# Four graph layers over sorted edges: record loads by several steps, stores of end rows by four, a relation loop with six buffers

## The chip, the cores and the metric

The kernel runs on one core of a Trainium2 chip. The metric is the device time of one execution in microseconds (us), the median over several executions. Beside it stands one profiled execution, whose records say what each engine did and waited for. Engines are named as in the profile: PE (TensorE, matmuls), DVE (VectorE), ACT (ScalarE), POOL (GpSimd) and SP (SyncE); PEq, SPq, ACTq are their instruction queues.

## The reference

A graph has 3125 nodes with 256 features and 103125 edges (50000 in both directions and a loop at each node). Four layers follow each other, each on `h = relu(layernorm(x))` and each added to `x`:

```python
x = x + _L0_gnn_ref(h, edge_index, edge_attr_18, ...)            # 16 heads; k and q get a projection of the attributes
x = x + _L1_gnn_ref(h, edge_attr_64, edge_weight, edge_index, ...)  # 8 heads, edge projection, then a feed-forward block
x = x + _L2_gnn_ref(h, weight, gamma, beta, src, dst, edge_type_8)
x = x + _L3_gnn_ref(h, src, dst, W, attn_l, attn_r, bias)        # 4 heads, additive attention, leaky relu
```

Layers 0, 1 and 3 are attention: for every edge a score per head from both ends' rows, a softmax over the edges that share a node, and the sum of the weighted value rows over those edges. Layer 2 is a sum without softmax, then a batch norm:

```python
all_h = jnp.einsum('ni,rio->nro', h, weight)      # eight relations: a table of 8 rows per node
msg = all_h[src, rel]
agg = jax.ops.segment_sum(msg, dst, num_segments=h.shape[0])
```

## The kernel before

**Stages.** The kernel sorts the edges on the chip by source and by destination and writes a *record* for each into two lists in memory, `by_src_records` and `by_dst_records` (node numbers, table index, attributes, weight). Then come, one after the other with a barrier of all engines between them: the layer loops `edges0` (over the list by source), `edges1`, the relation loop and `edges3` (over the list by destination), and between them stages that join the sums, project `x` and write the tables of the next layer. All loops have their instructions in program order on each engine; semaphores alone tie the engines together, and there is no planner.

**A step.** The sorted list has T = 856 tiles of 128 edges, and a step is G = 8 tiles, so that each loop has STEPS = 107 steps. Two tiles are a pair; a step has PAIRS = 4. Nodes lie in blocks of BN = 126 rows, NB = 25 blocks, joined in GROUPS = 5 groups of 5. A pair's edges belong to one block of nodes, whose number DVE loads into a register (`blocks_of`).

**Relation loop (`relation_sums`).** SP loads the step's records (L1684, 128 partitions x 8 tiles x 8 words). POOL gathers, tile by tile, 128 rows of 256 values from the table `rel` into `rows` (L1693, eight indirect DMAs a step). DVE makes eight one-hot matrices 128x128 from the records (L1724). PE multiplies, two tiles into one PSUM bank for each pair (L1709, 8 matmuls a step), and DVE adds the pair's PSUM to `acc` (printed as `agg`, L1741). The order is kept by these semaphores: `rec_in[b]` (records there), `gathered[b][h]` (half a step's rows there), `hot_ready` (one-hots there), `summed` (PE, one increment per pair) and `added` (DVE, one per pair). With BUFS2 = 3 buffers SP waits at step n, before it loads, until `summed` says that step n - 3 is finished. POOL waits for nothing but `rec_in`, so its buffer of rows is guarded through SP's wait. PE waits before each pair's matmuls until DVE has added the pair three before, since the PSUM banks are four.

**Layer loops (`edge_layer`, kind 0, 1, 3).** The same outline with more work: SP loads the records (L1137) into `rec`, one of BUFS = 4 buffers, after `score_done` of the step four before; POOL gathers rows of keys and values (L1152) when the records are there and PE has finished the step four before; ACT, DVE and PE make one-hots, scores, exponentials and weighted rows; PE sums them by pairs (L1262, kind 1 L1273); ACT copies the sums out of PSUM (L1411, L1415, in `move_sums`), and once a step stores the two *end rows* of each pair, which belong to nodes that the next block of edges also has, into `ends` (L1418), having waited with `ends_out` for the store before. The loops are unrolled by 12 steps.

**Others.** In the sort, SP loads the attributes of each step (L539) into the records that POOL then scatters. After it, SP loads the segment words of the first and the last edge of each tile (L920, 28 DMAs). In each joining stage SP loads the sums of segments that were cut between tiles, `far`, block by block (L1844 in `load_parts`, 25 DMAs of 128 rows; 126 of them are the block's, the last two those of the next).

## Time and profile before

| what | us |
|---|---|
| median of 3 executions | 9863.49 (9828.07 to 9897.71) |
| the profiled execution | 9902.93 |
| its span in the profile | 9901.2 |
| edges0, edges1, relation loop, edges3 (stretches) | 1720, 1549, 1299, 1354 |
| busy over the span: PE, DVE, POOL, ACT | 6502.3, 5118.9, 5166.4, 3754.8 |

The stages can't overlap, so each loop's length is set by the engine or the wait that ends last in it, and the busy times over the whole span say little. "Idle before" in a row is the time that the engine stood still just before the instruction; what ended it is inferred from semaphore events, and a wait for a *count* of a semaphore (as `summed` is) can be put down to a wrong instruction, here several times to "DMA edges_kv<-kv,edges_rec", a gather of an earlier stage. "issue" is idle time that ended with nothing that the profile shows. The granted clock of PE was 0.779 over the span; 0.5 is 1.2 GHz and 1.0 is 2.4 GHz.

### The profile page before, as it was taken

To read this page: it belongs to the slowest core of one execution; us is meant where nothing else is said; L and a number is where in the kernel's file an instruction comes from. 1 tells how busy PE (TensorE), PEld (TensorE's weight loads), DVE (VectorE), ACT (ScalarE), POOL (GpSimd) and SP (SyncE) were. 2 spreads that over 40 slices of the span, in tenths; PEclk is the share of its full clock that TensorE was granted. 3 is DMA by queue.
4 is the path that set the end of the run, shared out by engine and by line. 5 is a ranking of instruction groups with operands and counts; after the bars stand their busy time and mean duration, and the time that the engine had idled before them with its cause. 6 is when DMAs were issued, how large, how long until landed. Compare 5 with 4: busy or idle time off the path is not lost. (4 is left out here: it accounts for less than half of the span.)

```text
span 9901.2 us, 144141 instructions
## 1 busy us (share of the span) xinstructions
PE 6502.3 (66%) x32549; PEld 4796.2 (48%) x32550; DVE 5118.9 (52%) x15163; ACT 3754.8 (38%) x11176; POOL 5166.4 (52%) x5189
## 2 busy tenths in 40 slices
PE   8555555666556777777578888879644545566664
PEld 7554444445444555555356655656433334344443
DVE  6665555555545555565577777741122223344445
ACT  3221112222224555555266666744100001566663
POOL 0565555666655445555156656530366663566664
PEclk9666766666768889899789999989766666677776
DMA  7310002111114334444255555542333333333333
GB/s 222 88 13 12 13 12 60 27 27 27 26 23 106 101 103 105 107 108 105 91 156 157 158 152 161 161 113 65 85 91 90 88 90 71 85 89 88 89 90 75
DMA packets 1047506, 873.99 MB, mean 88 GB/s; under 512 B 755175, under 2 KB 863893, under 8 KB 1046843
## 3 DMA queue, kind: packets, MB, share of 16 engines
q0 software_dynamic: 259600, 655.15, 24.4%
q1 hardware_dynamic: 731943, 158.23, 8.2%
q10 hardware_dynamic: 55428, 54.63, 1.7%
q8 instruction: 195, 3.19, 0.1%
q14 instruction: 340, 2.79, 0.1%
HBM read 733.43 MB, written 134.17 MB: 88 GB/s over the span
## 5 line engine op out<-in xcount | busy, mean ns | idle before, releaser
L1152 POOL DMA_INDIRECT edges_kv<-kv,edges_rec x1712 | 1826.7, 1067 | 1474.7 <-issue 728.1
L1262 PE MATMUL banks<-edges_kv,edges_hot 128*128 128x288 f32 (+2 forms) x5136 | 1716.7, 489 | 739.5 <-DVE edges_kv L1536 630.5
L1262 PEld LDWEIGHTS banks<-edges_kv,edges_hot 128*128 128x128 f32 x5136 | 1159.5, 236 | 1121.9 <-ACT edges_pair_sums L1415 344.1
L558 POOL DMA_INDIRECT by_src_records<-sort_by_src_rec,sort_pos_i x808 | 783.1, 969 | 801.9 <-DVE sort_pos_i L625 553.6
L699 PE MATMUL banks<-sort_table,sort_hot_hi_t 128*128 128x128 f32 x3232 | 862.9, 405 | 422.1 <-DVE sort_junk L643 246.7
L1693 POOL DMA_INDIRECT edges_rows<-rel,edges_rec x856 | 810.3, 947 | 588.8 <-DMA edges_rec<-by_dst_records 319.8
L1152 POOL DMA_INDIRECT edges_kv<-feat,edges_rec x856 | 821.7, 960 | 538.9 <-issue 329.9
L1709 PE MATMUL banks<-edges_rows,edges_hot 128*128 128x256 f32 x1712 | 624.2, 530 | 678.2 <-DVE agg L1741 284.8
L558 POOL DMA_INDIRECT by_dst_records<-sort_by_dst_rec,sort_pos_i x808 | 783.1, 969 | 541.1 <-DVE sort_pos_i L625 329.9
L643 DVE SCALAR_TENSOR_TENSOR sort_junk<-banks,sort_hot_lo 128x128 bf16<-128x128 f32 x1616 | 439.0, 286 | 1083.4 <-remote 737.5
L699 PEld LDWEIGHTS banks<-sort_table,sort_hot_hi_t 128*128 128x128 f32 x3232 | 670.8, 284 | 504.6 <-DVE sort_junk L643 290.2
L1709 PEld LDWEIGHTS banks<-edges_rows,edges_hot 128*128 128x128 f32 x1712 | 433.0, 265 | 869.5 <-issue 420.1
L1380 ACT ACTIVATE edges_off<-columns,edges_column 128x128 bf16<-128x128 f32 x2568 | 784.5, 390 | 0.0
L577 ACT COPY sort_hot_hi_t<-banks 25x512 f32<-25x512 f32 x404 | 232.3, 575 | 1335.2 <-remote 732.6
L1352 ACT ACTIVATE edges_apart<-banks,minus_p 128x512 bf16<-128x512 f32 x642 | 429.8, 686 | 700.5 <-DMA sort_feat<-in_edge_attr_dram 298.8
L1741 DVE TENSOR_TENSOR agg<-banks,agg 128x256 f32 x428 | 181.1, 423 | 986.1 <-DMA edges_kv<-kv,edges_rec 541.7
L694 PE MATMUL banks<-sort_hot_lo,sort_hot_hi 128*128 128x128 bf16 x1616 | 293.1, 277 | 530.1 <-ACT sort_table L598 515.0
L635 DVE SCALAR_TENSOR_TENSOR sort_junk<-banks,sort_key_cur,sort_earlier 128x128 bf16<-128x128 f32 x1616 | 576.3, 412 | 5.8 <-PE banks L678 5.8
L1569 DVE TENSOR_TENSOR edges_kv<-banks,edges_kv 128x256 f32<-128x256 f32 (+1 forms) x856 | 448.9, 553 | 186.3 <-remote 84.5
L1222 PE MATMUL banks<-x,edges_hot_t 128*128 x1712 | 496.6, 415 | 54.8 <-issue 41.0
L1554 DVE TENSOR_TENSOR edges_kv<-banks,edges_kv 128x256 f32<-128x256 f32 x428 | 179.1, 420 | 673.2 <-PE banks L1222 403.9
L1536 DVE TENSOR_TENSOR edges_kv<-edges_kv 128x1024 f32<-128x1024 f32 x428 | 519.8, 1215 | 3.9 <-ACT edges_kv L1397 3.9
(438 smaller groups left out, 12933.3 us busy)
## 6 DMA issues: line engine op xcount, KB each, us to landing
edges_kv<-kv,edges_rec POOLq DMA_INDIRECT x1712
sort_feat<-in_edge_attr_dram SPq DMA_DIRECT2D x100, 256.0 KB, 3.3
rel<-tables_stage SPq DMA_DIRECT2D x100, 252.0 KB
by_dst_records<-by_dst_blank ACTq DMA_DIRECT2D x1, 17120.0 KB
edges_rec<-by_dst_records SPq DMA_DIRECT2D x107, 160.0 KB
edges_rows<-rel,edges_rec POOLq DMA_INDIRECT x856
edges_kv<-feat,edges_rec POOLq DMA_INDIRECT x856
by_src_records<-sort_by_src_rec,sort_pos_i POOLq DMA_INDIRECT x808
```

Of the source, the lines that this page charges most:

```text
L558: pool.indirect_dma_start(O.rec, bass.IndirectOffsetOnAxis(ap=pos_i[:, b, c:c + 1], axis=0), rec[:, b, c, :], None).then_inc(scattered[b], 16)
L635: last = dve.scalar_tensor_tensor(out=junk[:, c, 0:P + mates].rearrange("p (t e) -> p t e", e=P), in0=ps[:, 4 + h, end - P - mates:end].re ...
L643: dve.scalar_tensor_tensor(out=junk[:, c, 2 * P:3 * P], in0=ps[:, 2 + c % 2, 0:P], scalar=1.0, in1=hot_lo[:, u, c, :], op0=ALU.mult, op1=A ...
L699: pe.matmul(ps[:, 2 + c % 2, 0:P], hot_hi_t[:, u, c, :], table[:, d % 2, :], start=True, stop=True).then_inc(looked_up, 1)
L1152: pool.indirect_dma_start(kv[:, r, c, 0:koff + DIM], None, tab, bass.IndirectOffsetOnAxis(ap=reci[:, r, c, idx:idx + 1], axis=0)).then_inc ...
L1222: last = pe.matmul(out[:, c, 2 * P - QW:2 * P], hot_t[:, b % 2, 2 * m + c, :], rows, start=(kind == 1), stop=(kind == 1 or c == 1), skip_g ...
L1262: last = pe.matmul(ps[:, 6 + m % 2, 0:OW], hot[:, b % 2, c, :], kv[:, b % BUFS, c, koff:koff + OW], start=(c % 2 == 0), stop=(kind != 1 an ...
L1380: last = act.activation(off[:, c, :], C.columns[:, c % 2, :], ACT.Abs, bias=column[:, b % 2, c:c + 1], scale=-1.0)
L1536: dve.tensor_tensor(v4, v4, bc(exps, dh), ALU.mult).then_inc(msg_done, 1)
L1569: dve.tensor_tensor(k2, by, k2, ALU.mult).then_inc(edges_used, 1)
L1693: pool.indirect_dma_start(rows[:, b, c, :], None, tab, bass.IndirectOffsetOnAxis(ap=reci[:, b, c, idx:idx + 1], axis=0)).then_inc(gathered ...
L1709: last = pe.matmul(ps[:, m, 0:DIM], hot[:, b, c, :], rows[:, b, c, :], start=(c % 2 == 0), stop=(c % 2 == 1))
```

## The change

- **Relation loop.** BUFS2 goes from 3 to 6, so that `rec` and `rows` hold six steps. SP loads the records of three steps in one DMA (LOAD = 3), for a group whose first step is n as soon as step n - 4 is finished (`n + 3 - 6` steps counted). PE increments `step_summed` once a step in place of `summed` once a pair, and waits for `added` once a step: three sets of PSUM (`sum_of`: two pairs in one bank, six banks) stand where four banks stood. The one-hots have three sets (SETS) and DVE makes them two steps ahead.
- **Layer loops.** `rec` holds twelve steps, loaded four at once (LOAD = 4). `pair_sums` holds four steps (HELD = 4), and the end rows of four steps are stored in one DMA.
- **Sort.** The attributes of two steps are loaded by one DMA, after a wait for both steps' scatters.
- **Head columns.** 10 DMAs in place of 28.
- **Joins.** `load_parts` loads a group's five blocks with one DMA of 126 partitions; POOL clears partitions 96 to 127 of `far` beforehand.

```diff
-BUFS, BUFS2 = 4, 3
+BUFS, BUFS2 = 4, 6
...
-                        for tile, q, lag in ((K.seg_head, 0, 0), (K.seg_prev, P - 1, 1)):
...
-                                sp.dma_start(tile[p0:p0 + last - first, k:k + 1],
-                                             seg_word[q, first:last].rearrange("(t o) -> t o", o=1)).then_inc(head_in[i], 16)
+                        whole = (TB - 1) * P
+                        sp.dma_start(K.seg_head[:, 0:TB - 1], seg_word[0, 0:whole].rearrange("(k p) -> p k", p=P)).then_inc(head_in[i], 16)
+                        sp.dma_start(K.seg_head[0:TLAST, TB - 1:TB], seg_word[0, whole:T].rearrange("(t o) -> t o", o=1)).then_inc(head_in[i], 16)
+                        sp.dma_start(K.seg_prev[1:P, 0:1], seg_word[P - 1, 0:P - 1].rearrange("(t o) -> t o", o=1)).then_inc(head_in[i], 16)
+                        sp.dma_start(K.seg_prev[:, 1:TB - 1], seg_word[P - 1, P - 1:whole - 1].rearrange("(k p) -> p k", p=P)).then_inc(head_in[i], 16)
+                        sp.dma_start(K.seg_prev[0:TLAST, TB - 1:TB], seg_word[P - 1, whole - 1:T - 1].rearrange("(t o) -> t o", o=1)).then_inc(head_in[i], 16)
...
     LO_BANKS = (3, 3) if kind < 3 else (3, 2)
     SEG_BANK = {0: 4, 1: 0, 3: 5}[kind]
     UNROLL = 12
+    LOAD = 4
     ENDS = 96
+    HELD = 4
     ROUNDS = -(-STEPS // UNROLL)
...
-        rec = ph.sbuf("rec", [P, BUFS, G, RW])
+        rec = ph.sbuf("rec", [P, UNROLL, G, RW])
...
-        pair_sums = ph.sbuf("pair_sums", [P, PAIRS, OW])
+        pair_sums = ph.sbuf("pair_sums", [P, HELD, PAIRS, OW])
...
-                    if not first_steps(j, b, BUFS):
-                        sp.wait_ge(score_done, at(j, b)(1, 1) - BUFS)
-                    sp.dma_start(rec[:, b % BUFS], records[:, bass.ds(j * (UNROLL * G) + b * G, G), word0:O.width]).then_inc(rec_in[b % BUFS], 16)
+                    if b % LOAD:
+                        return
+                    some = min(LOAD, size(j) - b)
+                    if not first_steps(j, b, UNROLL):
+                        sp.wait_ge(score_done, at(j, b)(1, some) - UNROLL)
+                    sp.dma_start(rec[:, b:b + some].rearrange("p s c w -> p (s c) w"),
+                                 records[:, bass.ds(j * (UNROLL * G) + b * G, some * G), word0:O.width]).then_inc(rec_in[b // LOAD], 16)
...
-                    pool.wait_ge(rec_in[r], turn_of(j, b) * 16 + 16)
+                    pool.wait_ge(rec_in[b // LOAD], j * 16 + 16)
...
-                    if 0 in pairs:
-                        act.wait_ge(ends_out, n(16, 0))
+                    if 0 in pairs and b % HELD == 0:
+                        act.wait_ge(ends_out, j * (UNROLL // HELD * 16) + b // HELD * 16)
...
-                    if PAIRS - 1 in pairs:
+                        act.copy(pair_sums[:, b % HELD, m, :], ps[:, 6 + m % 2, 0:OW]).then_inc(sums_copied, 1)
+                    if PAIRS - 1 in pairs and (b % HELD == HELD - 1 or b == size(j) - 1):
+                        held = b % HELD + 1
                         act.wait_ge(sums_copied, n(PAIRS, PAIRS))
-                        act.dma_start(ends_rows[:, bass.ds(n(PAIRS, 0), PAIRS), :], pair_sums[BN:P]).then_inc(ends_out, 16)
+                        act.dma_start(ends_rows[:, bass.ds(at(j, b + 1 - held)(PAIRS, 0), held * PAIRS), :],
+                                      pair_sums[BN:P, 0:held].rearrange("p s m w -> p (s m) w")).then_inc(ends_out, 16)
...
+    SETS = 3
+    LOAD = 3
+    IOTA = 7
...
+    def opening(j, b, n):
+
+        return isinstance(j, int) and j * BUFS + b < n
...
+    def sum_of(b, m):
+
+        return ps[:, 2 * (b % SETS) + m // 2, DIM * (m % 2):DIM * (m % 2) + DIM]
...
-                    sp.wait_ge(summed, (j * BUFS + b) * PAIRS - (BUFS - 1) * PAIRS) if not (isinstance(j, int) and j == 0) else None
-                    sp.dma_start(rec[:, b], records[:, bass.ds(j * (BUFS * G) + b * G, G), word0:O.width]).then_inc(rec_in[b], 16)
+                    if b % LOAD:
+                        return
+                    some = min(LOAD, (FINAL if isinstance(j, int) and j == ROUNDS - 1 else BUFS) - b)
+                    if not opening(j, b, BUFS):
+                        sp.wait_ge(step_summed, at(j, b)(1, some) - BUFS)
+                    sp.dma_start(rec[:, b:b + some].rearrange("p s c w -> p (s c) w"),
+                                 records[:, bass.ds(j * (BUFS * G) + b * G, some * G), word0:O.width]).then_inc(rec_in[b // LOAD], 16)
...
                     n = at(j, b)
+                    if not opening(j, b, SETS):
+                        pe.wait_ge(added, n(PAIRS, 0) - (SETS - 1) * PAIRS)
                     pe.wait_ge(hot_ready, n(1, 1))
                     for m in range(PAIRS):
                         if m % 2 == 0:
                             pe.wait_ge(gathered[b][m // 2], j * 64 + 64)
-                        if not (isinstance(j, int) and j == 0 and b == 0):
-                            pe.wait_ge(added, n(PAIRS, m) - (PAIRS - 1))
                         for c in (2 * m, 2 * m + 1):
-                            last = pe.matmul(ps[:, m, 0:DIM], hot[:, b, c, :], rows[:, b, c, :],
+                            last = pe.matmul(sum_of(b, m), hot[:, b % SETS, c, :], rows[:, b, c, :],
                                              start=(c % 2 == 0), stop=(c % 2 == 1))
-                        last.then_inc(summed, 1)
+                    last.then_inc(step_summed, 1)
...
                 def one_hot(j, b):
 
-                    if not (isinstance(j, int) and j == 0):
-                        dve.wait_ge(summed, at(j, b)(PAIRS, 0) - (BUFS - 1) * PAIRS)
-                    dve.wait_ge(rec_in[b], j * 16 + 16)
-                    dve.tensor_tensor(hot[:, b], ps[:, 7, 0:P].unsqueeze(1).to_broadcast([P, G, P]), bc(rec[:, b, :, lo], P),
+                    if not opening(j, b, SETS):
+                        dve.wait_ge(step_summed, at(j, b)(1, 1) - SETS)
...
+                one_hot(0, 1)
...
                 def body(j, b, ahead):
                     n = at(j, b)
+                    beyond = None
                     if ahead:
-                        one_hot(*ahead)
+                        beyond = (ahead[0], ahead[1] + 1) if ahead[1] < BUFS - 1 else (ahead[0] + 1, 0)
+                        if isinstance(beyond[0], int) and beyond[0] * BUFS + beyond[1] >= STEPS:
+                            beyond = None
+                    if beyond:
+                        one_hot(*beyond)
                     blocks = blocks_of(dve, O, j, b, BUFS)
+                    dve.wait_ge(step_summed, n(1, 1))
                     for m in range(PAIRS):
-                        dve.wait_ge(summed, n(PAIRS, m + 1))
-                        if not (isinstance(j, int) and j == 0 and b == 0 and m == 0):
+                        if not (opening(j, b, 1) and m == 0):
                             dve.wait_ge(added, n(PAIRS, m))
                         part = acc[:, bass.ds(blocks[m], 1), :].rearrange("p o w -> p (o w)")
-                        dve.tensor_tensor(part, ps[:, m, 0:DIM], part, ALU.add).then_inc(added, 1)
+                        dve.tensor_tensor(part, sum_of(b, m), part, ALU.add).then_inc(added, 1)
...
+    sp.wait_ge(S.far_cleared, 1)
     for g in range(GROUPS):
-        for b in members(g):
-            sp.dma_start(S.far[:, b, :], S.far_dram[b * BN:b * BN + P, :]).then_inc(S.far_in[g], 16)
+        rows = S.far_dram[GROUP * g * BN:GROUP * (g + 1) * BN, :]
+        sp.dma_start(S.far[0:BN, group_of(g), :], rows.rearrange("(b p) w -> p b w", p=BN)).then_inc(S.far_in[g], 16)
...
-    dve.wait_ge(S.far_in[g], 16 * GROUP)
+    dve.wait_ge(S.far_in[g], 16)
...
+            pool.wait_ge(S.dump_ready, 2)
+            pool.memset(S.far[96:P], 0.0).then_inc(S.far_cleared, 1)
+            pool.wait_ge(S.far_cleared, 1)
```

What is left out follows the same edits (`rec[:, b]` for `rec[:, b % BUFS]`, `pair_sums[:, b % HELD, ...]`), and the attributes of the sort. In the rows below a semaphore is printed by the name under which its number was first used.

**SP at the start of the relation loop.** Before, `sort_sums` is `summed`:

```order
243 L1684 DMA edges_rec<-by_dst_records 128x8x8 x3
244 L95 UNCONDITIONAL_BRANCH
245 L95 ISA
246 L1684 ISA [waits sort_sums]
247 L1684 DMA edges_rec<-by_dst_records 128x8x8
248 L1683 ISA
249 L1684 ISA [waits sort_sums]
250 L1684 DMA edges_rec<-by_dst_records 128x8x8
```

After, `sort_feat_last` is `step_summed`:

```order
177 L1712 DMA edges_rec<-by_dst_records 128x24x8 x2
178 L95 UNCONDITIONAL_BRANCH
179 L95 ISA
180 L1712 ISA [waits sort_feat_last]
181 L1712 DMA edges_rec<-by_dst_records 128x24x8
182 L1712 ISA [waits sort_feat_last]
183 L1712 DMA edges_rec<-by_dst_records 128x24x8
```

The first loads are two of three steps each in place of three of one, and a turn of the loop, which is six steps now and was three, has two waits and two loads; it had three of each.

**PE in the relation loop.** Before (`sort_feat_in0` is `added`, `sort_hist_used` is `hot_ready`, `sort_loaded0` to `2` are `gathered`):

```order
5125 L1705 ISA [waits sort_hist_used]
5126 L1707 ISA [waits sort_loaded0]
5127 L1709 MATMUL banks<-edges_rows,edges_hot 128x256 [waits sort_feat_in0]
5128 L1709 MATMUL banks<-edges_rows,edges_hot 128x256
5129 L1707 REGISTER_ALU
5130 L1709 MATMUL banks<-edges_rows,edges_hot 128x256 [waits sort_feat_in0]
5131 L1709 MATMUL banks<-edges_rows,edges_hot 128x256
5132 L1707 REGISTER_ALU [waits sort_loaded1]
5133 L1709 MATMUL banks<-edges_rows,edges_hot 128x256 [waits sort_feat_in0]
5134 L1709 MATMUL banks<-edges_rows,edges_hot 128x256
5135 L1709 MATMUL banks<-edges_rows,edges_hot 128x256 [waits sort_feat_in0]
```

After (`sort_feat_turned` is `added`, `sort_feat_in3` is `hot_ready`, `sort_duo_in` and `sort_loaded0` to `2` are `gathered`):

```order
5129 L1733 ISA [waits sort_feat_turned]
5130 L1736 ISA [waits sort_feat_in3]
5131 L1738 MATMUL banks<-edges_rows,edges_hot 128x256 [waits sort_duo_in]
5132 L1738 MATMUL banks<-edges_rows,edges_hot 128x256 x3
5133 L1738 MATMUL banks<-edges_rows,edges_hot 128x256 [waits sort_loaded0]
5134 L1738 MATMUL banks<-edges_rows,edges_hot 128x256 x3
5135 L1732 REGISTER_ALU
5136 L1733 REGISTER_ALU [waits sort_feat_turned]
5137 L1738 MATMUL banks<-edges_rows,edges_hot 128x256 [waits sort_loaded1,sort_feat_in3]
```

The wait for `added` stood ahead of each pair's two matmuls; now it stands once ahead of the step's eight.

**DVE in the relation loop.** Before, from the last adds of the first step to the second step's first (`sort_feat_in0` is `added`, `sort_sums` is `summed`, `sort_duo_in` is `rec_in`):

```order
2995 L1741 REGISTER_ALU [waits sort_feat_in0,sort_sums]
2996 L1741 REGISTER_ALU
2997 L1741 ISA
2998 L1741 TENSOR_TENSOR agg<-banks,agg 128x256
2999 L1741 REGISTER_ALU [waits sort_feat_in0,sort_sums]
3000 L1741 REGISTER_ALU
3001 L1741 ISA
3002 L1741 TENSOR_TENSOR agg<-banks,agg 128x256
3003 L1724 TENSOR_TENSOR edges_hot<-banks,edges_rec 128x1024 [waits sort_duo_in]
3004 L982 TENSOR_LOAD by_dst_duo_block
3005 L1741 REGISTER_ALU [waits sort_feat_in0,sort_sums]
```

After, the same place (`sort_feat_turned` is `added`, `sort_feat_last` is `step_summed`, `sort_x_in` is `rec_in`):

```order
2996 L1776 REGISTER_ALU [waits sort_feat_turned]
2997 L1776 REGISTER_ALU
2998 L1776 ISA
2999 L1776 TENSOR_TENSOR agg<-banks,agg 128x256
3000 L1776 REGISTER_ALU [waits sort_feat_turned]
3001 L1776 REGISTER_ALU
3002 L1776 ISA
3003 L1776 TENSOR_TENSOR agg<-banks,agg 128x256
3004 L1753 TENSOR_TENSOR edges_hot<-banks,edges_rec 128x1024 [waits sort_x_in,sort_feat_last]
3005 L988 TENSOR_LOAD by_dst_duo_block
3006 L1776 REGISTER_ALU [waits sort_feat_turned,sort_feat_last]
```

The waits for PE's sums between a step's adds are gone, and one ahead of the step is left; the one-hots still stand between two steps' adds, now for the step after the next.

## Rows read from the trace of the kernel before

**Rows 1.** Stretches of the stages: busy us (instructions) of each engine, PEclk, DMA share, GB/s.

```profile
4939.00:6488.00 1549.00, 1270.41 (x5579) 923.15 (x5580) 1172.56 (x1691) 1025.13 (x2728) 948.05 (x855) 0.92 0.58 157
...
7025.00:8324.00 1299.00, 624.18 (x1712) 433.04 (x1712) 306.47 (x537) 0.00 (x0) 810.31 (x856) 0.65 0.36 89
```

**Rows 2.** Waits in the relation loop, 7050 to 8270: total us, times, longest.

```profile
DVE agg L1741 <- DMA edges_kv<-kv,edges_rec: 516.4, 74, 10.2
...
POOL edges_rows L1693 <- issue: 256.2, 785, 4.4
...
POOL edges_rows L1693 <- DMA edges_rec<-by_dst_records: 196.0, 27, 8.5
```

**Rows 3.** Gathers in the same stretch: busy us, mean ns, idle before them.

```profile
L1693 POOL DMA_INDIRECT edges_rows<-rel,edges_rec x812 | 768.6, 947 | 452.2 <-issue 256.2 <-DMA edges_rec<-by_dst_records 196.0
```

**Rows 4.** Timeline, 7504 to 7548: start, us, engine, line, operation, [idle before].

```profile
7506.68 33.02 SPq L1684 DMA_DIRECT2D edges_rec<-by_dst_records  x4
...
7509.61 0.94 POOL L1693 DMA_INDIRECT edges_rows<-rel,edges_rec  x1 [7.24 <-DMA edges_rec<-by_dst_records]
...
7516.36 1.99 PE L1709 MATMUL banks<-edges_rows,edges_hot 128*128 128x256 f32 x8 [1.19 <-DMA edges_rows<-rel,edges_rec]
...
7521.27 2.53 PE L1709 MATMUL banks<-edges_rows,edges_hot 128*128 128x256 f32 x8 [2.92 <-DMA edges_rows<-rel,edges_rec]
7521.91 0.43 DVE L1741 TENSOR_TENSOR agg<-banks,agg 128x256 f32 x1 [3.78 <-DMA edges_kv<-kv,edges_rec]
...
7528.94 0.42 DVE L1741 TENSOR_TENSOR agg<-banks,agg 128x256 f32 x1 [6.60 <-PE banks L1709]
...
7538.39 0.95 POOL L1693 DMA_INDIRECT edges_rows<-rel,edges_rec  x1 [0.30 <-issue]
7539.44 0.42 DVE L1741 TENSOR_TENSOR agg<-banks,agg 128x256 f32 x1 [10.07 <-DMA edges_kv<-kv,edges_rec]
...
7542.49 0.95 POOL L1693 DMA_INDIRECT edges_rows<-rel,edges_rec  x1 [3.15 <-issue]
```

**Rows 5.** Waits of the whole stage, 7025 to 8324.

```profile
POOL edges_rows L1693 <- DMA edges_rec<-by_dst_records: 319.8, 29, 118.2
```

**Rows 6.** Timeline at the stage's start.

```profile
7025.28 1.65 SPq L1684 DMA_DIRECT2D edges_rec<-by_dst_records  x3
...
7028.31 1.02 POOL L1693 DMA_INDIRECT edges_rows<-rel,edges_rec  x1 [118.16 <-DMA edges_rec<-by_dst_records]
```

**Rows 7.** DMA view inside edges1, 5000 to 6400.

```profile
q1 hardware_dynamic: 100880, 15.90, 6.5%
...
edges_rec<-by_dst_records SPq DMA_DIRECT2D x97, 160.0 KB
```

**Rows 8.** Waits of GpSimd in the same stretch.

```profile
POOL edges_kv L1152 <- PE banks L1273: 240.2, 68, 11.9
```

**Rows 9.** Waits of VectorE in the same stretch.

```profile
DVE edges_kv L1559 <- DMA edges_kv<-kv,edges_rec: 27.8, 24, 2.2
```

**Rows 10.** Waits of ScalarE in the same stretch.

```profile
ACT edges_apart L1352 <- ACT edges_pair_sums L1411: 58.8, 80, 0.8
```

**Rows 11.** The store of the end rows: duration min/median/max, first and last start.

```profile
L1418 ACTq DMA_DIRECT2D ends<-edges_pair_sums x321: 243/244/491, 3048.2 to 9794.1; - x161
```

**Rows 12.** SyncE's issues for the head columns.

```profile
2948.52 3.15 SPq L920 DMA_DIRECT2D sort_by_src_head<-by_src_records  x7
...
2959.34 3.35 SPq L920 DMA_DIRECT2D sort_by_dst_prev<-by_dst_records  x7
```

**Rows 13.** Timeline in the last stage, 9800 to 9856.

```profile
9802.76 22.13 POOL L2915 TENSOR_TENSOR x<-x,combine_bias 128x1280 f32<-128x1280 f32 x5 [5.11 <-DMA combine_bias<-in_L_gnn_bias_dram]
...
9847.33 8.88 SPq L1844 DMA_DIRECT2D combine_far<-far  x19
9851.61 0.18 DVE L1885 TENSOR_TENSOR combine_most<-combine_far,acc 128x20 f32<-128x20 f32 x1 [21.19 <-DMA combine_far<-far]
```

**Rows 14.** The page, costliest groups: busy us, mean ns, idle before, releaser.

```profile
L558 POOL DMA_INDIRECT by_src_records<-sort_by_src_rec,sort_pos_i x808 | 783.1, 969 | 801.9 <-DVE sort_pos_i L625 553.6
```

68 lines of the change are left out of this document (36 added, 32 removed).

## The prediction

> **What bounds the kernel now.** I read the table of the stages' stretches first, since the stages can't overlap. In the relation loop no engine is full: of 1299 us PE works 624, DVE 306, POOL 810, and the DMA engines are busy 0.36 of the time [rows 1]. So waits set its length, and the next view is that of the waits between 7050 and 8270 us. POOL's 812 gathers there are busy 768.6 us [rows 3]; 256.2 us lie between gathers with nothing waited for, about 0.30 us each, and 196.0 us in 27 waits for records [rows 2]. The three make 1220.8, the whole stretch: POOL never stops for anything else. The stage ends with POOL's last gather and some 15 us behind it, so POOL's stream sets its length. The reader should see that the record load itself is short. From SP's first issue to POOL's first gather pass 3.03 us [rows 6], and where POOL stood 7.24 us before 7509.61, SP had issued at 7506.68, 2.93 us earlier [rows 4]. The rest is SP's own wait for `summed`.
>
> Why is `summed` late? The timeline shows a chain that the named releasers hide [rows 4]. PE works on a step's last two pairs from 7521.27 to 7523.80. DVE's adds, each of which waits for one increment of `summed`, run at 7521.91, 7528.94 and 7539.44, and the last is 15.6 us behind the matmul it waited for. DVE had nothing else to do (10.07 us idle before it, put down to a gather of an earlier stage). So PE's increments are seen late while POOL gathers, and in that piece about one comes every 7.0 to 10.5 us, mean 8.8. At 7539.44 POOL had begun its last gather 1.05 us before and stood still; then DVE goes on, and SP with it, and POOL starts again at 7542.49.
>
> A step of POOL is 8 x (768.6 + 256.2) / 812 = 10.1 us [rows 2, 3]. Four increments a step at one per 8.8 us can't keep up with it; POOL has to run dry from time to time.
>
> **Relation loop.** What is removed: three of four increments and DVE's three waits for them, PE's wait for `added` at each pair, two of three record loads. What is added: three buffers, so more distance.
>
> The distance before: SP loads step n when step n - 3 is summed, so two steps of POOL, 20.2 us, lie between the last gather of step n - 3 and the first of n. Off it go 2.9 us for the load and the way from the last gather to the end of PE's matmuls: that gather ends at 7509.61 + 7 x 1.262 + 0.95 = 7519.4, PE at 7523.80, so 4.4 us [rows 4]. 12.9 us are left, less than the 15.6 us by which the increment was late. After: a group's load waits for step n - 4, so the distance is 30.3 - 7.3 = 23 us, and one increment a step at 8.8 us keeps pace with a step of 10.1. At the slow end of what the piece shows, 10.5 us, the lag would grow by 0.4 us a step and use up 23 us in some 55 steps. I take four stops left in 107 steps, of the present mean of 196.0 / 27 = 7.3 us: 29 us.
>
> What can be gained at most: all waits for records in the stage are 319.8 us in 29, of which 118.2 are the wait before the stage's first gather [rows 5], so 201.6. Gain: 201.6 - 29 = 173, **-173 us**. From below the bound is a gain of nothing and a loss (the rival below), from above 201.6 and another 10 from the long ones (4.4 us) among the "issue" gaps, -212. I take a value near the upper end, since the loop then has 23 us of room against a measured 15.6.
>
> What is late next? PE needs for eight matmuls, halves of 1.99 and 2.53 us, 4.5 us a step [rows 4], and 624.18 / 107 = 5.8 us in the mean [rows 1], DVE 306.47 / 107 = 2.9. Both are below 10.1, so POOL's own issue is what is left. DVE's new wait for `step_summed` ahead of a step's four adds has the next one-hot queued behind it, and PE waits for that; but the one-hot is now made two steps ahead, so PE has its own for some 20 us. PE's wait for `added` looks back two steps and one pair's add, about as far.
>
> The Trainium skill's page "TensorE: Matmul & The Clock Gate", section "The cost: per-tile semaphore tail", says that completion increments are written one after the other, 26.3 ns each, and that one on the last is enough. By it three fewer a step would be worth 3 x 26.3 ns x 107, an estimate of 8 us, and the lateness would not exist. The rows show delays of microseconds where it speaks of nanoseconds, so the trace does not agree.
>
> **Start of the loops.** The first load brings three or four steps instead of one. In the relation loop a load of one step landed 3.03 us after its issue [rows 6]; four times the data in edges1 is at most what four loads take. There one step's load of 160 KB [rows 7] is 6.5% of 16 DMA engines for a step of 1400 / 97 = 14.4 us, so 0.94 us a step, and three more steps 2.8 us. I take 1.5 us for each of four loops, **+6** (0 to +11).
>
> **Layer loops, records.** POOL there waits for PE's sums (240.2 us in 68 waits) and for no record [rows 8], since its value buffers stay four. Loading sooner brings nothing: the gathers hide it, and if that cover is gone a wait of 3 us at each group is its price. I cost it at **0**; the bursts are a rival below.
>
> **End rows.** A store costs ACT 0.244 us of its queue [rows 11] and a wait for the last pair's copy, after which ACT starts on the next one-hots (0.7 us each, 58.8 us in 80 waits) [rows 10]. Of 107 stores per layer 27 stay. If all of both were on the path, 3 x 80 x (0.244 + 0.735 x 0.6) would be 160 us; but in edges1 ACT works 1025 us of 1549 and DVE 1173 [rows 1], and POOL waits for PE, so most of it falls into idle time. The nearest row for the path is the store alone, 3 x 80 x 0.244 = 59 us. I take a quarter, **-15** (0 to -60).
>
> **Head columns.** SP issues 28 DMAs from 2948.52 to 2962.69, 14.2 us [rows 12], and the next stage waits for the last. Ten at 0.5 us are 5 us. Larger ones of 768 single words land later, perhaps 1 to 2 us: **-8** (0 to -9).
>
> **Joins.** The first group's five loads land 4.28 us after the first issue (9847.33 to 9851.61), 19 issues take 8.88 us [rows 13]. One DMA per group issues in 0.5, but has five blocks' data in one: 2 us sooner for the last groups, which DVE's work on the group before hides. POOL's clearing of `far` stands ahead of its adds of the bias (22.13 us from 9802.76, so done at 9824.89) [rows 13], and the loads come 22 us after these, so 7 us more are covered; were they not, each of three stages would be 7 us longer. **-3** in all (-8 to +20).
>
> The Trainium skill's page "DMA: Bandwidth & Descriptors", section "Why a DMA increments its semaphore by 16 and not by 1", speaks against this part: a transfer uses the largest number of engines up to 16 that divides its slowest dimension, so 126 rows would go over 14 engines and 128 over 16. By it the loads would be a seventh slower, an estimate of under 1 us a stage; no row of before shows such a load.
>
> **Sort.** Loads by two steps: POOL's scatters there wait for DVE's positions (553.6 of 801.9 us idle) [rows 14], **0** (-5 to +10).
>
> **Sum.** -173 + 6 + 0 - 15 - 8 - 3 = -193. The profiled execution, 9902.93 us with a span of 9901.2, lies 39 us above the median of 9863.49; the same difference from the median gives 9863 - 193 = **9670**.
>
> **Rivals.**
> *The increments stay late.* If it isn't their number that delays them but POOL's stream itself, fewer don't come sooner, and only the buffers help: POOL runs dry once in six steps. 107 / 6 = 18 stops x 7.3 = 131 us, so 70 are gained, and the sum is -90: 9773. For it: the last three adds lie 7.0 and 10.5 us apart whatever PE does. Against: the lag measured is less than the new distance.
> *Bursts.* A record load of four steps goes through the same 16 engines as the gathers. In edges1 it is 4 x 0.94 = 3.8 us of all of them [rows 7], and one step's part of it is there now. If each burst held POOL's gathers by its excess of 2.8 us once in four steps, 27 x 2.8 = 76 us, and with edges0 and edges3, which have 96 and 32 KB and somewhat less time for each, up to 184. With the gain: -193 + 184, about 9855. DVE does wait for gathers in edges1, but 27.8 us in 24 waits only [rows 9], and the sources of the wait are the sums, which speaks for slack.
> *Slower.* The increments pass only once POOL stops. The row at 7539.44, an increment that comes 1.05 us after POOL's last gather has begun, can be read so. Then SP's load comes at every group: 107 / 3 = 35 stops, each 7.3 us and about 1 more for a load of three steps, 291 us in place of 201.6: +89, and with the other terms (-20) +69: 9932. It decides as soon as the lag of one increment is over 23 us.
>
> **Chances.** Forecast 0.65, increments stay late 0.17, bursts 0.12, slower 0.06. Forecast and first rival hold 0.82, their bounds are -265 and about -60, so 9595 to 9805; I put the upper end at 9815 for the half of the bursts. A difference under 1% (99 us) can't be told from none here. The first rival lies at that edge, so half of it counts as the same: faster 0.73, same 0.21, slower 0.06.
>
> **What the changed profile would show.** The relation loop near 1125 us, POOL's waits for records in a handful, gathers 1.25 us apart nearly throughout; DVE's add ahead of a step at most 20 us behind PE's last matmul. Waits for records at every sixth step would be the first rival, at every third the last. Edges0, 1 and 3 within 10 us of now, with fewer stores; more than 20 us longer with DVE or PE waiting for gathers would be the bursts. The prediction is wrong if PE's increments lag more than 23 us with one a step, or if the layer loops, whose step is set by sums and not by loads, change with the number of their DMAs.

## The result, and the profile after

| | median us | range | executions |
|---|---|---|---|
| before | 9870.53 | 9801.64 to 9910.24 | 20 |
| changed | 9826.72 | 9776.17 to 9869.29 | 20 |

The ratio is 0.9943, 95% interval 0.9925 to 0.9961: a gain of 44 us where 193 were forecast; 9826.72 lies above the upper end of the range, 9815. The profiled execution of the changed kernel has a span of 9823.2 us and a granted clock of 0.776.

The stretches of edges1 and of the relation loop (start to end; busy us and instructions of PE, PEld, DVE, ACT, POOL; clock, DMA share, GB/s) answer to [rows 1]:

```profile
4905.00:6412.00 1507.00, 1264.06 (x5589) 920.42 (x5590) 1170.41 (x1693) 1033.93 (x2737) 954.86 (x856) 0.94 0.60 162
6956.00:8231.00 1275.00, 594.41 (x1678) 408.93 (x1679) 294.56 (x514) 0.00 (x0) 811.34 (x856) 0.66 0.37 90
```

The stretch of edges1 is 42 us shorter in this pair of profiles (1549 and 1507), which by itself says little: the changed kernel's edges1 took 1551 us from its first to its last gather in run 5 below and 1507 here.

The relation loop, forecast to shrink to 1125 us, takes 1275 us from its first to its last gather; it took 1281.0. The waits between 7000 and 8200 us in that loop, which answer to [rows 2], say how:

```profile
DVE agg L1776 <- DMA tables_far<-far: 567.8, 37, 36.9
...
POOL edges_rows L1722 <- issue: 239.2, 779, 2.1
...
POOL edges_rows L1722 <- DMA edges_rec<-by_dst_records: 206.7, 18, 12.2
```

POOL still waits 206.7 us for records in this stretch, in 18 waits where 27 waits took 196.0. There are fewer and longer stops. Over the whole loop it is 206.7 us in 18 for 201.7 in 28; the 6 us that the loop is shorter by come out of POOL's gaps put down to "issue", 256.9 us for 269.0, of which seven were longer than 1 us before (19.1 us in all) and one is now. The spacing of the gathers is the same. DVE's idle time, again put down to a transfer of an earlier stage, has waits of up to 36.9 us; the longest was 10.2.

One period of 72 us, in the timeline of all engines (start, duration, engine, line, operation, count, [idle before]), answers to [rows 4]:

```profile
7111.11 3.44 PE L1738 MATMUL banks<-edges_rows,edges_hot 128*128 128x256 f32 x8 [3.35 <-DMA edges_rows<-rel,edges_rec]
...
7112.33 0.42 DVE L1776 TENSOR_TENSOR agg<-banks,agg 128x256 f32 x1 [2.83 <-issue]
...
7115.52 1.97 PE L1738 MATMUL banks<-edges_rows,edges_hot 128*128 128x256 f32 x8 [0.97 <-DMA edges_rows<-rel,edges_rec]
...
7120.47 3.40 PE L1738 MATMUL banks<-edges_rows,edges_hot 128*128 128x256 f32 x8 [2.99 <-DMA edges_rows<-rel,edges_rec]
...
7125.58 1.97 PE L1738 MATMUL banks<-edges_rows,edges_hot 128*128 128x256 f32 x8 [1.71 <-DMA edges_rows<-rel,edges_rec]
...
7130.48 1.03 PE L1738 MATMUL banks<-edges_rows,edges_hot 128*128 128x256 f32 x3 [2.93 <-DMA edges_rows<-rel,edges_rec]
...
7131.89 0.29 PEld L1738 LDWEIGHTS banks<-edges_rows,edges_hot 128*128 128x128 f32 x1 [0.91 <-issue]
...
7133.29 0.58 PE L1738 MATMUL banks<-edges_rows,edges_hot 128*128 128x256 f32 x1 [1.78 <-issue]
...
7134.69 0.29 PEld L1738 LDWEIGHTS banks<-edges_rows,edges_hot 128*128 128x128 f32 x1 [2.51 <-issue]
...
7136.10 0.59 PE L1738 MATMUL banks<-edges_rows,edges_hot 128*128 128x256 f32 x1 [2.23 <-issue]
...
7143.40 0.42 DVE L1776 TENSOR_TENSOR agg<-banks,agg 128x256 f32 x1 [26.25 <-DMA tables_far<-far]
...
7157.72 0.95 POOL L1722 DMA_INDIRECT edges_rows<-rel,edges_rec  x1 [0.30 <-issue]
...
7164.80 0.59 PE L1738 MATMUL banks<-edges_rows,edges_hot 128*128 128x256 f32 x1 [0.82 <-issue]
...
7166.19 3.57 PE L1738 MATMUL banks<-edges_rows,edges_hot 128*128 128x256 f32 x8 [0.80 <-issue]
...
7166.54 0.42 DVE L1776 TENSOR_TENSOR agg<-banks,agg 128x256 f32 x1 [19.42 <-DMA tables_far<-far]
7166.57 0.37 SPq L1712 DMA_DIRECT2D edges_rec<-by_dst_records  x1
...
7170.68 0.94 POOL L1722 DMA_INDIRECT edges_rows<-rel,edges_rec  x1 [12.02 <-DMA edges_rec<-by_dst_records]
```

The reader should see three things. First, PE does whole half-steps at once until 7130 (8 records in 2 to 3.5 us), but the adds that wait for the last matmul of 7111.11 to 7114.55 come at 7143.40, 28.9 us later, and those of the next step, whose last matmul ended at 7123.87, at 7166.54, 42.7 us later. Second, from 7131.89 on PE itself moves in single instructions, a weight load or a matmul mostly every 1.40 us, with nothing that it waits for. (The whole loop has 249 such steps of 1.40 us, and 77 of 0.70 and 21 of about 2.1 between them; the loop before has 3 of 1.40.) Third, POOL's last gather begins at 7157.72, and only at 7166.19 PE goes on at speed; at 7166.54 DVE adds, at 7166.57 SP loads the records and at 7170.68 POOL restarts, 12.02 us after it stopped.

For the head columns SP issues its ten loads from 2919.48 to 2924.58, 5.1 us for 14.2 as forecast, and the way from the last scatter to the first gather of edges0 is 30.6 us for 35.8, so 5 us shorter where 8 were forecast.

### The profile page after: what moved, and what is told of

It reads as the page before. It is cut to its first block and busy times, and to the rows that moved or that the text cites. A ratio compares the mean times of both kernels' runs of the same rounds, so it can differ in the third digit from the quotient of the medians.

```text
span 9823.2 us, 140985 instructions
## 1 busy us (share of the span) xinstructions
PE 6503.9 (66%) x32549; PEld 4804.2 (49%) x32550; DVE 5122.6 (52%) x15163; ACT 3750.0 (38%) x11176; POOL 5197.7 (53%) x5192
## 5 line engine op out<-in xcount | busy, mean ns | idle before, releaser
L1738 PE MATMUL banks<-edges_rows,edges_hot 128*128 128x256 f32 x1712 | 604.2, 500 | 694.9 <-issue 417.8
```

What stands on the lines that cost most here:

```text
L1738: last = pe.matmul(sum_of(b, m), hot[:, b % SETS, c, :], rows[:, b, c, :], start=(c % 2 == 0), stop=(c % 2 == 1))
```

## Experiments

**Two conditions.** The kernel before was run beside the others in each of six sets of runs. It took 8210.73, 8220.9 and 8216.87 us in three sets and 10142.77, 10105.25 and 9881.6 in three others. The condition lasts through a whole set, and it isn't tied to a chip: one chip had 8220.9 in one set and 10105.25 in the next. The forecast and the measurement above are of the second kind. I call the first *free* and the second *held*, after what the traces show below. Ratios are always within a set.

Two obvious causes can be looked for in the relation loop's records. The granted clock is lower there when held (0.66 before, 0.75 in run 1), but one matmul record takes 530 ns in the mean for 531; and a gather lands 2.56 us after its start for 2.57. So by these records neither the clock nor slower transfers make the difference.

**1. The relation loop alone (free).** The kernel before with the edits of `relation_sums` and BUFS2 only:

```diff
-BUFS, BUFS2 = 4, 3
+BUFS, BUFS2 = 4, 6
... and the hunks of relation_sums as in the change; all else as before
```

> The kernel before with the change of the relation loop alone. The changed kernel's profile shows 18 stops of 11.7 us there, about 203 us as before. If the relation loop has nothing left to give, this kernel's loop from the first to the last gather is 1275 us, as in the changed kernel (1281 before), and the whole is within 15 us of before; the 44 us of the changed kernel then come from elsewhere. If the relation loop gives the 44 us after all, this kernel is 40 us faster and the loop near 1240.

Measured: 8218.79 us, ratio 1.0006 (0.9996 to 1.0016). Its relation loop (stretch, as above) and the waits in it:

```profile
5807.00:6877.00 1070.00, 620.51 (x1696) 427.80 (x1696) 305.93 (x528) 0.00 (x0) 809.17 (x856) 0.75 0.44 107
```

```profile
DVE agg L1763 <- PE banks L1725: 634.8, 102, 8.2
...
POOL edges_rows L1709 <- issue: 248.8, 817, 0.3
```

There is no wait for records at all: 856 gathers in 1069.8 us, each 0.30 us behind the last. The new loop reaches the floor that the forecast's 1.262 us a gather gives (856 x 1.262 = 1080 us), which neither of the two expected outcomes had, as both took the held condition for granted, and since the whole is no faster than before, the old loop, not profiled in this condition, can't have stopped for long either. So three buffers and four increments a step are enough when increments come at once.

**2 to 4. Twelve buffers, a break, a probe (free).**

```diff
-BUFS, BUFS2 = 4, 6
+BUFS, BUFS2 = 4, 12            # run 2
```

> The changed kernel with BUFS2 = 12. Theory A, PE's increments are only late, and room covers it: one stop in 12 steps of the same 11.7 us, 9 stops, 105 us in place of 203, loop 1177, the whole 98 us under the changed kernel. Theory B, PE and VectorE fall behind during POOL's stream because each of their handovers takes 20 to 40 us while they are only three steps of PSUM apart: POOL's stop is then the time in which they catch up what they missed, and it grows with the steps in the stream: 9 stops of 20 us and more, loop within 30 us of 1275. Rival C, the increments come within some 60 us by themselves: no stop, loop 1075.

```diff
+                    pool.wait_ge(paused, at(j, b)(1, 0))     # before a step's gathers; run 3
+                    pool.memset(idle[:], 0.0).then_inc(paused, 1)   # 128 x 1200, after them
```

> The changed kernel with a clear of 1200 values per partition on POOL after each step's eight gathers, about 1 us in which POOL issues no gather. If a backlog of POOL's gathers holds PE's increments and a short break drains it, the increments come promptly, POOL's waits for records vanish, and the loop is 1072 + 107 x 1.3 = 1210, 65 us under the changed kernel. If a short break doesn't drain it, the stops stay at 18 of 11.7 us less some of the pause, and the loop is between 1275 and 1275 + 139 = 1414.

```diff
+                        if m == 1:
+                            last.then_inc(half_summed, 1)    # run 4
                     last.then_inc(step_summed, 1)
+                    pe.sem_inc(pe_mark, 1)
... and ScalarE: act.wait_ge(hot_ready, n(1, 1)); act.copy(mark[:], C.iota[:]).then_inc(act_mark, 1)
```

> The changed kernel with marks on semaphores of their own: TensorE also increments one with the step's second pair of matmuls and one with an instruction of its sequencer behind the step, and ScalarE, idle in this loop, copies 128 x 128 values after each one-hot and increments one. If only increments that come with a matmul are held, the sequencer's and ScalarE's are seen within 0.5 us while the matmuls' take 20 to 40. If all of TensorE's are held, the sequencer's are late too and ScalarE's are not. If all engines' but GpSimd's are held, all are late.

Measured: 8293.56 us (1.0098, 1.0081 to 1.0115), 8465.41 (1.0306, 1.0289 to 1.0323), 8284.24 in one execution. No loop stopped for records (1069.7, 1250.5 and 1069.7 us), so these three say nothing of lateness. They do say two things of the free condition: the break costs 181 us in 107 steps, 1.7 us each where I had expected 1.3, and the changed kernel is slower than before in this condition (seen on these variants; it was not run here itself). Its relation loop isn't the reason, since run 1 has it.

**5 to 8. Parts of the change for the layer loops (held).** Run 5 is the changed kernel. Run 6 is the kernel before with `HELD = 4` and records step by step; run 7 the reverse:

```diff
-    LOAD = 4
+    LOAD = 1        # run 6, on the layer hunks alone
-    HELD = 4
+    HELD = 1        # run 7, on the layer hunks alone
```

Run 8 is the changed kernel with two sets of end-row buffers:

```diff
-    HELD = 4
+    HELD, KEPT = 2, 4
-                        act.wait_ge(ends_out, j * (UNROLL // HELD * 16) + b // HELD * 16)
+                        if not first_steps(j, b, KEPT):
+                            act.wait_ge(ends_out[b // HELD % 2], j * (UNROLL // KEPT * 16) + b // KEPT * 16)
```

> The changed kernel itself, to be compared on the same chip with those below. The first runs came from a chip on which the kernel before takes 8210.73 us, where no increment of TensorE was late (in the relation loop POOL waited for no record). If this call comes to such a chip: 8270 to 8290, 0.7 to 1.0% slower than before, edges1 50 us longer. If it comes to one where the kernel before takes about 9870: 0.5% faster.

> The kernel before with end rows of four steps stored at once (HELD = 4); records are still loaded step by step, but into twelve buffers. In the twelve-buffer run ScalarE waited 33.8 us in 18 waits for the store of the end rows inside edges1, where the relation-only kernel waited 4.0 in 2, since the store of four steps is begun when the next step's copy is due and its only buffer holds all four. Theory S: that wait is what makes edges1 50 us longer; this kernel has edges1's gathers at 1380 to 1400 us where the relation-only kernel had 1339. Theory L, it is the bursts of the grouped loads: edges1 stays at 1339.

> The kernel before with records of four steps in one load (LOAD = 4), end rows stored step by step. Theory S: edges1 stays within 10 us of 1339. Theory L (VectorE's waits for gathers in edges1 were 73.8 us in 60 against 35.9 in 40): edges1 40 to 60 us longer, edges0 and edges3 7 each.

> The changed kernel with end rows of two steps stored at once from two sets of buffers (the same memory as one set of four), so that the copy of the next step waits only for the store before the last. Theory S: the wait for the stores falls from 34 to under 5 us in edges1, and the whole is 40 to 60 us under the changed kernel. Theory L: within 10 us of the changed kernel.

Measured: run 5 10112.96 us, ratio 0.9960 (0.9932 to 0.9988); run 6 10097.05, 0.9962 (0.9933 to 0.9991); run 7 10158.18, 1.0004 (0.9977 to 1.0030); run 8 10103.6, 0.9965 (0.9936 to 0.9993). The end rows alone give as much as the whole change within the noise, grouped records nothing that can be told from none. Two sets of end rows give nothing more, so this condition doesn't decide between theories S and L; the wait for the store was short here anyway (8.7 us in edges1 in run 5, none in run 8). Single profiles can't split this by stage here: the first scatter stage, whose code is the same in runs 6 and 7 and before, took 1378 and 1466 us in them.

**9 to 12. The probe, more increments, twelve buffers, the break (free again).**

> The probe once more (TensorE also increments a semaphore with the step's second pair and one with an instruction of its sequencer; ScalarE increments one), since the chip of its first run held no increment back. Where TensorE's increments are held (kernel before near 9870 or 10140): if only increments that come with a matmul are held, the sequencer's and ScalarE's are seen within 0.5 us; if all of TensorE's are, the sequencer's are late too and ScalarE's not. In the profiles so far one increment passes per 10 us of stream in the kernel before, which makes four a step, and one per 45 us in the changed one, which makes one. If the passes go with the number that TensorE makes, this kernel, with three a step, shows one per 12 to 20 us.

```diff
+                        if m < PAIRS - 1:
+                            last.then_inc(pair_summed, 1)    # run 10
                     last.then_inc(step_summed, 1)
```

> The changed kernel where TensorE also increments a semaphore that nobody waits for with each of a step's first three pairs, so four increments a step as before. Theory P, an increment is let through by those made after it: step_summed passes within 10 us, POOL's stops shrink below 100 us in sum, and the kernel is some 100 us under the changed one. Theory Q, each increment takes its turn of about 10 us: three more ahead of it make a step's 40 us late, and the loop is as in the changed kernel, 1275 to 1290, or longer.

> The changed kernel with BUFS2 = 12, on a chip where increments are late. Theory A, room covers lateness: 9 stops of 10 us, the loop 1160 to 1190, 0.9% under the changed kernel. Theory B, TensorE and VectorE fall behind in the stream (a step's handover takes some 45 us there, a step of POOL 10), and a stop is as long as the catching up: 9 stops of 20 us or more, loop 1260 to 1290, no change of the whole.

> The changed kernel with 1 us of clearing on POOL after each step's gathers, on a chip where increments are late. On the other chip this cost 180 us in 107 breaks, 1.7 us each, with no stop before and none after (loop 1250.5 against 1069.7). If a short break lets the increments through, the loop is 1250 here too, 25 to 40 us shorter than the changed kernel's. If not, its stops come on top: 1350 to 1450.

Measured: 8294.17 us in one execution; 8296.73 (1.0097, 1.0081 to 1.0114); 8304.0 (1.0102, 1.0085 to 1.0119); 8477.1 (1.0312, 1.0295 to 1.0329). They repeat runs 2 to 4 on another chip, and each loop is again without a stop.

**13 and 14. Runs 6 and 7 again (held).**

> The kernel before with end rows of four steps stored at once, alone. On a chip without late increments (kernel before 8210 to 8220) theory S has edges1 at 1380 to 1400 us from the first to the last gather (1338.8 without, 1388 to 1400 with the whole change) and the kernel 50 to 70 us slower than before; theory L has it at 1339. On a chip with late ones: 0.4% faster than before, as measured there once.

> The kernel before with the records of four steps in one load, alone. Without late increments theory L has edges1 at 1380 to 1400 and the kernel 50 to 70 us slower; theory S within 10 us of 1339 and the kernel within 0.2%. With late ones: no change, as measured there once.

Measured: 10084.59 us, 0.9966 (0.9932 to 1.0000); 10094.11 us, 0.9982 (0.9950 to 1.0014). As in runs 6 and 7.

**15. Twelve buffers with marks (held).** Run 2 with the marks of run 4, without `half_summed`.

> The changed kernel with BUFS2 = 12, a mark on a semaphore of its own by TensorE's sequencer after each step, and one by ScalarE. With late increments: theory A (room covers lateness) 9 stops of 10 us, loop 1160 to 1190; theory B (handovers of 45 us a step in the stream make TensorE and VectorE fall behind, and the stop is their catching up) stops of 20 us and more, loop 1260 to 1290. Marks: ScalarE's within 0.5 us; TensorE's sequencer's late if all of TensorE's increments are held, prompt if only those that come with a matmul are. Without late increments: loop 1070, all marks prompt.

Measured: 10088.34 us, 0.9968 (0.9937 to 0.9999). Its relation loop takes 1275.6 us, as with six buffers, and POOL's wait for records between 7230 and 8430 is

```profile
POOL edges_rows L1725 <- DMA edges_rec<-by_dst_records: 197.2, 18, 22.7
```

with single stops of up to 22.7 us. Room doesn't cover the lateness: theory A is out. Theory B has the loop right but not the stops, which are not 9 of 20 us and more but 19 of 10.8 in the mean over the whole loop. From the same trace's records of semaphores I counted how long before each count that was seen the last increment of its kind had been made. Where a count belongs to an earlier increment, the true delay is longer, so the last column is a lower bound; the longest is 43 us. Records of some counts are missing:

```
who increments            made  seen   within 0.5 us   later (median)
POOL, sequencer             98    65        65          0
DVE, one-hot                91    52        52          0
DVE, add                   366   254       254          0
ACT, mark                   91    50        50          0
PE, sequencer's mark        93    74        74          0
PE, with a matmul           93    84        24         60 (18.0 us)
```

Only the increments that come with a matmul are late. In run 9, in the free condition, none is missing and all of each kind in the loop, 107 a kind and 428 of the adds, came within 0.5 us. The missing records are themselves a mark of the held condition: of the 107 counts of the one-hots, for example, 107 are there in run 9, 68 in the kernel before and 66 in the changed one. Whether the recording of the profile has a part in the lateness was not tested.

**16 and 17. More increments, and a break (held).** Run 16 is run 10 with LOAD = 1 in the layer loops, run 17 is run 3 with HELD = 1 there; the layer parts were for the free condition.

> Two independent stages in one kernel, so that it tells something in either condition. The changed kernel with the layer loops' records loaded step by step (LOAD = 1), end rows still by four, and in the relation loop the three more increments a step that nobody waits for. Without late increments (before at 8220): theory S, edges1 at 1380 to 1400 us, as slow as the whole change; theory L, 1339. With late ones (before at 9870 to 10110): theory P, step_summed is pushed through by the increments behind it, loop 1180; theory Q, no better, 1275 to 1290 or longer.

> The changed kernel with the end rows stored step by step (HELD = 1), records still by four, and in the relation loop the break of 1 us on POOL after each step. Without late increments: theory S, edges1 within 10 us of 1339; theory L, 1380 to 1400; the relation loop 1250. With late ones: if the increments are held only when POOL issues without a break, loop 1250 with no stop for records, 25 us under the changed kernel; if the stop must last some 8 us to let them through (as the profile shows them 8.5 us after a last gather began), stops of 7 us and more stay on top of the breaks, loop 1350 to 1450.

Measured, run 16: 9826.71 us, 0.9942 (0.9919 to 0.9965), relation loop 1277.1 us with 19 stops. Of the waited increments one passed per 44.8 us of unbroken stream (counted from 12 us after a stream's start to its last gather; 18 counts); it was 44.9 in the changed kernel (18 counts), and one of four a step per 10.3 in the kernel before. Theory P is out, since four increments a step don't come sooner than one, and theory Q too: a fixed time of some 10 us for each increment can't give 44.9 us where there is one a step. The passes go with the work. In each case it is about one *step* per 41 to 45 us.

Run 17: 9836.85 us, 0.9945 (0.9913 to 0.9978), relation loop 1250.2 us, 25 us under the changed kernel's, with no stop for records. The waits on POOL from 7000 to 8200 (the 121.2 us are the wait for the stage to begin), and one break in the timeline:

```profile
POOL edges_rows L1726 <- issue: 234.2, 721, 1.3
POOL edges_rows L1726 <- DMA edges_rec<-by_dst_records: 121.2, 1, 121.2
POOL edges_rows L1726 <- POOL edges_idle L1729: 71.8, 91, 0.8
```

```profile
7302.59 0.95 POOL L1726 DMA_INDIRECT edges_rows<-rel,edges_rec  x1 [0.30 <-issue]
7303.53 1.11 POOL L1729 MEMSET edges_idle<- 128x1200 f32 x1
7305.44 0.95 POOL L1726 DMA_INDIRECT edges_rows<-rel,edges_rec  x1 [0.80 <-issue]
```

The break makes two gathers start 2.85 us apart where it is 1.25 otherwise. With it 106 of 107 matmul increments were seen within 0.5 us, and PE has 4 steps of 1.40 us in the loop for 249. Not the distance and not the number of increments cured the lateness, but 1.6 us in each 11.6 in which POOL issues no gather. The whole kernel's ratio, 0.9945, can't tell these 25 us from the changed kernel's 0.9943 or 0.9960.

**18. A shorter break, and two sets of end rows (free).** Run 8 with the break of run 17, clearing 64 values for 1200:

> The version that the runs point to: the changed kernel with a break on POOL after each step of the relation loop that clears 64 values instead of 1200 (about 0.7 us longer between two gathers instead of 1.6), and with end rows of two steps stored at once from two sets. With late increments: if so short a break is enough, no stop for records, the loop at 1071 + 107 x 0.7 = 1146 us, 130 us under the changed kernel's 1275, and the whole 0.9870 to 0.9800 of before; if it's too short, stops come back and the loop lies between 1250 and 1350, the whole at 0.995 to 1.003. Without late increments: loop 1146 where it would be 1070, and edges1 at 1345 by theory S (the store of end rows is what costs it), at 1390 by theory L (the grouped loads).

Measured: 8367.78 us, 1.0180 (1.0166 to 1.0194), relation loop 1152.5 us, 0.77 us a break. Whether 0.77 us is enough in the held condition was not told; there the loop would be 1152 and not 1250 if it is. Edges1 is the other result. The waits in edges1, from 4000 us to its end, of the kernel with the old layer loops (run 1), of the changed layer loops (run 10), and of run 18:

```profile
POOL edges_kv L1152 <- PE banks L1273: 143.7, 68, 9.6
...
DVE edges_kv L1559 <- DMA edges_kv<-kv,edges_rec: 35.9, 40, 2.8
...
ACT acc L1409 <- DMA ends<-edges_pair_sums: 4.0, 2, 2.4
```

```profile
POOL edges_kv L1164 <- PE banks L1285: 180.8, 68, 11.3
...
DVE edges_kv L1572 <- DMA edges_kv<-kv,edges_rec: 69.8, 55, 2.4
...
ACT acc L1420 <- DMA ends<-edges_pair_sums: 37.0, 21, 2.5
```

```profile
POOL edges_kv L1164 <- PE banks L1285: 162.0, 60, 11.7
...
DVE edges_kv L1575 <- DMA edges_kv<-kv,edges_rec: 73.3, 63, 3.2
```

The wait for the store of end rows, 37.0 us with the one set of four, is gone with two sets of two, but edges1 only falls from 1394.0 to 1387.5 us, and run 4, which has the one set, took 1387.9 (1387.9 to 1400.0 in the seven runs that have it); with the old loops it is 1338.8. So the store on its own is not what makes edges1 50 us longer, and theory S has fallen. What stays from the change in that loop are the grouped records with their twelve buffers, and DVE's waits for gathers have doubled (35.9 to 73.3 us). The records of DMA packets agree: in run 1 a load of one step takes 3.6 us from SP's issue to its last packet, and gathers begun meanwhile land 3.51 us after their start, others 3.55; in run 18 a load of four takes 7.7 us, and gathers begun meanwhile take 4.27, others 3.59. Runs 2, 4, 9 and 10 have 4.25 to 4.32 beside 3.56 to 3.60. No run had the grouped load alone in the free condition, so this is by elimination and by that delay, not by a run that undoes it.

## Why the prediction was wrong

**The bound of the relation loop** was read rightly: POOL's gathers set its floor, and run 1 reaches it (1069.8 us). The waits for records are the only stops.

**The failed step** is "one increment a step at 8.8 us keeps pace with a step of 10.1", and with it "the loop then has 23 us of room against a measured 15.6". I took the 8.8 us for a price of an *increment*. It is a price of PE's *work*: an increment was let through per pair before, and one per step takes four times as long, 44.9 us. The rows had a sign of it: the add at 7521.91 comes 3.6 us behind its pair, whose matmuls end at 7516.36 + 1.99 = 7518.35, and the add two pairs later is 15.6 us behind [rows 4]. The lag was growing, and I took its last value for its size. The prediction's own sign of being wrong, a lag over 23 us with one increment a step, came: 28.9 and 42.7 us in the timeline. The late matmuls of the timeline give the size. When PE's queue is full it takes one instruction per 1.40 us, and a step is 16 weight loads and 16 matmul records: 32 x 1.40 = 44.8 us a step, 11.2 us a pair, beside 44.9 and 10.3 counted (with the steps of 0.70 and 2.1 among them the mean is 1.29, 41 us a step). That PE's instructions are *finished* at this pace throughout the held stretches is my reading of these three numbers; directly the trace shows the pace only where PE can't run ahead. Under it neither more buffers, nor fewer increments, nor PSUM for three steps can help, since PE owes the same instructions, and POOL has to stop for as long as PE needs to catch up. The sum of the stops is kept: 202, 207, 206 us with three, six and twelve buffers. Loops with the old code took 1281.0, 1293.8, 1295.8, 1292.4 and 1299.4 us in held profiles, with six buffers 1275.1, 1280.5, 1285.1 and 1277.1: means 1292.5 and 1279.5, a gain of 13 for -173. It is a gain of 6 in the first pair of profiles and of 12 in the set of runs 5 to 8; the other sets have no old and changed loop with six buffers side by side.

**The rivals.** "The increments stay late" came: its count of stops, once in six steps or 18, is what the profile shows (18), but its price took the length of a stop from before, 7.3 us. It was 11.5 (206.7 / 18), since more is to be caught up. With that the rival would have stood at 9863 - (202 - 207) - 20, about 9848. That the count fits owes something to luck: with twelve buffers the stops are 19 again and not 9. "Bursts" is real in the free condition, where edges1 is 50 us longer; in the held one it is hidden (runs 7 and 14 are level with before), since a slower PE is waited for anyway (that reason is argued, not shown). Its upper figure of 184 us doesn't come out of its rows: by the sizes of the loads it is 76 x (1 + 0.6 + 0.2) = 137 us, which gives about 9807 for 9855. The slower rival's condition, a lag over 23 us, was met, but the stop at every third step that it was to bring didn't come. And the lower bound of -265 is not the sum of the terms' lower ends, which is -299.

**The other terms.** End rows: -15 forecast; run 6 gives -38 us (0.38% of 10142.77, interval 0.09 to 0.67%) and run 13 -34 (0.34%, 0 to 0.68%), so mis-sized within its own bounds; how fewer stores save it the profiles don't tell. Head columns: -8, and 5 us in the first pair (35.5 to about 30 us in the free condition); that larger loads would land 1 to 2 us later, no run shows by itself. Starts of the loops: +6, and from SP's first load of records to POOL's first gather it is 3.5 to 5.8, 4.9 to 7.1, 3.0 to 4.4 and 3.0 to 5.7 us in the four loops, +9 in all. Joins: -3, and from SP's first load of `far` to the next loop's first gather it is 171.7 to 174.1 us ahead of edges1 and 460.7 to 463.8 ahead of the relation loop, 53.9 to 54.0 to the kernel's end: 6 us longer, of which 4 are the starts just named, so +2. Sort: 0, and the two scatter stages take 2057 us in run 1 and 2057 to 2063 with the change, both free; the held profiles, 1325 to 1466 us for the first stage alone, can't tell. Put together with the relation term as measured, -13 - 38 - 5 + 9 + 2 = -45, beside -44. That it meets so closely is luck, since the end rows alone are uncertain by 29 us.

## What to carry to other kernels

A count that is seen late can be late because of the increment, because of the way to it, or because the work behind it retires late; before giving it room, find out whether the lag is constant, or grows with the room and with the work per increment. Here a row where the engine moves in equal small steps with nothing to wait for told more than the waits did. Where a stream on one engine slows another, a short regular break in the stream can do what buffers don't (here 25 us of the held loop, at a price of 181 us in the free one, so it was no gain for this kernel), and an idle time that a slow engine hides (the bursts) comes back where that engine is quick, so a change should be weighed in both conditions.

## What the hardware showed that was not expected

- While POOL issued gathers 1.25 us apart without a break, and until about 8.5 us after the last began, increments that come with a matmul were seen up to 39.5 and 43.0 us late in two kernels (the changed one and run 15; medians of the late ones 11.6 and 18.0, as lower bounds); those of every other engine, and of PE's own sequencer, within 0.5 us. A break of 1.6 us in each step of 8 gathers removed it (106 of 107 within 0.5 us).
- This is so in one of two conditions of a chip, each of which lasted through all executions of a set of runs; in the other the same kernel takes 17 to 19% less time (8211 to 8221 us for 9871 to 10143). All of the difference lies in the stages in which POOL gathers or scatters: with the code of before the first scatter stage takes 1029 us in one (run 1) and 1353 to 1466 in the other (before, runs 6, 7, 13, 14), edges0 1300 and 1709, while the way between edges0 and edges1 takes 245 and 251, between edges1 and the relation loop 543 and 538. What sets the condition, and why gathers hold back PE's increments, no run here told.
